# Attention scores in 128 + 128 + 32 contraction rows, queries laid out from PSUM, high half of P copied from the f32 P

## The chip, the cores and the metric

The kernel runs on one core of a Trainium2 chip, as one launch. The metric is the device time of that launch in microseconds: a median over runs. For the kernel before it is 1063.67 us, of three runs between 1063.38 and 1064.74.

## What is computed

Two layers act on x (2 batches x 512 tokens x 1024, f32) with a context of 2 x 1024 x 1024: a quantised matmul with the context, a linear layer with a low-rank update, cross-attention with 16 query heads over 4 key heads, and a router with an expert bias. The change touches the attention alone, in which B = 2, 512 queries and 1536 keys (1024 of the context, 512 latents) per batch, KV = 4 key heads, G = 4 query heads for each of them, HD = 96:

```python
hidden = jnp.concatenate([context, latents], axis=1)
q = (latents @ Wq.T).reshape(b, q_len, H, HD)
k = (hidden @ Wk.T).reshape(b, s_len, KV, HD)
v = (hidden @ Wv.T).reshape(b, s_len, KV, HD)
...
scores = jnp.einsum('bkgqd,bksd->bkgqs', q, k) * scale
attn = jax.nn.softmax(scores.astype(jnp.float32), axis=-1).astype(q.dtype)
out = jnp.einsum('bkgqs,bksd->bkgqd', attn, v)
```

Every f32 matmul is made of f16 products: each operand is split into a high half (its f16 rounding) and a low half (what is left, as f16), and high x high, high x low and low x high are summed in PSUM.

## The kernel before

The five engines each run a program written out by hand, joined by semaphores. The first 333 us prepare context, the first layer, and the keys and values, which lie in DRAM scratch (`k_scratch` with high and low halves of K transposed, `v_scratch`). Then comes the attention loop, `for m in range(NU)` with NU = 128 units in 8 stages of 16. A stage t is one pair of key head and batch (g = t // 2, b = t % 2); a unit u = m % 16 within it is one tile of 128 queries (u // 4) and one query head (u % 4), against all 1536 keys. The whole order is by hand.

**TensorE** (loop at L860): per unit `scores(m)` (L787), then at most one side product into bank 7, then `weigh(m - LAG)` (L802), P·V of the unit three before, into bank 6. The scores of even units lie in banks 0 to 2, of odd units in 3 to 5. Scores are nine matmuls (L798) of 96 contraction rows and 512 columns: three combinations of halves in three banks. P·V is 24 matmuls (L813, L815): twelve of 192 columns, twelve of 96. Side products: half of a q product for the next stage, 12 matmuls (L772), at u = 4, 5, 8, 9, 10, 11, of which u = 5, 9 and 11 end a block j = 0, 1, 2; an output product, 9 matmuls, at u = 2, 3, 6, 7, 12 to 15; none at u = 0 and 1. In the first stage the q products are at u = 2 (whole), 4, 5, 7, 8, there are value products at u = 0 and 1, and output products only from u = 12. In the last stage there are no q products, and the router and expert work is put in. Before a side product, `side_free` (L848) waits until bank 7 has been read, for q on `q_free`, the subtraction of the low half.

**VectorE** (loop at L1648): per unit `row_max(m)` (L1558), the reciprocal of the row sum of m - 3 (L1562), `take_low_q` where a q block ended, `add_out` (L1552) where there was an output product, then `take_out(m - 3)` (L1572, L1574), which reads bank 6 after P·V and frees it: `weigh(m)` waits for `o_ok >= m`, that is for `take_out(m - 1)`.

**ScalarE** (loop at L1238): per unit the f32 exponential from PSUM into p32 (L1249, row sums on the side, `e32_ok`), `take_q` where a q block ended (L1191), the same exponential again from PSUM as f16, the high half p_hi (L1259, `exp_ok`), and copies of weights. **GpSimd** (loop at L1848): per unit p_lo = p32 - p_hi (L1723, `plo_ok`), plus low halves of weights at u = 7 to 10 and 12 to 15 of every other stage and of the outputs. **SyncE** (loop at L508): per unit the two transposing DMAs of P (L517, L519), and at u = 1 the loads of K (`load_k`, L446) and V (L451) of the next stage.

q comes out of its product as a block j of 128 rows: rows 0 to 95 are head j, rows 96 to 127 the j-th third of head 3 (`q_rows`, L301). `take_q` writes the high half of both parts, `take_low_q` (L1540) subtracts it from PSUM and writes the low half; both lie in `q_head[rows, batch, head, half, query]`. The scores wait for a whole stage of q (`q_free`), for K, and, from m = 2, for `exp_ok >= m - 1`: the unit before the last in the same banks has been read for the second time.

## Time and profile before

| | |
|---|---|
| median of the runs | 1063.67 us |
| the profiled execution, its own time | 1062.25 us |
| its span, first to last instruction | 1060.5 us |
| attention loop, about | 333 to 1036 us of the span |
| TensorE busy | 1038.3 us (98%) |
| VectorE, ScalarE, GpSimd busy | 641.5, 635.6, 644.3 us |

Times in rows are microseconds from the start of the span, except mean durations in ns. PE is TensorE, DVE is VectorE, ACT is ScalarE, POOL is GpSimd, SPq the queue of SyncE, which issues the DMAs. A matmul's recorded duration reaches beyond the start of the next one, since they are pipelined; the spacing of starts is what a matmul costs. A timeline row that says x9 covers nine instructions.

### The profile page before, as it was taken

What the parts mean: (1) busy time and instruction counts of PE and PEld (TensorE: products, weight loads), DVE (VectorE), ACT (ScalarE), POOL (GpSimd) and SP (SyncE); (2) the same over time, 40 slices, a digit from 0 to 9 for tenths busy, and PEclk for the clock granted to TensorE, in tenths of its full rate; (3) what the DMA queues carried; (4) which work ended last, traced back from release to release, by engine and by line L of the source; (5) the groups of instructions that cost most, each with busy time, mean ns of one, the idle gap of its engine ahead of it and who ended that gap; (6) DMA issues with size and microseconds to landing.
All of it is one profiled execution on the core that took longest, in us unless ns stands there. A gap on an engine that the chain in (4) does not pass through costs nothing.

```text
span 1060.5 us, 18394 instructions
## 1 busy us (share of the span) xinstructions
PE 1038.3 (98%) x7262; PEld 586.4 (55%) x7262; DVE 641.5 (60%) x1092; ACT 635.6 (60%) x711; POOL 644.3 (61%) x348
## 2 busy tenths in 40 slices
PE   9999999999999999999999999999999999998987
PEld 4555444444545556566665655656656565565553
DVE  6989849644223565556556655654655655566767
ACT  5686535431224687665667756657766566677764
POOL 4476778242001589666677865668866667687771
PEclk9999999999999999999999999999999999999999
DMA  9986664843223999999999999899999999999995
GB/s 339 257 306 214 199 212 116 183 81 60 73 88 106 163 214 213 208 214 160 193 179 198 165 234 174 159 210 173 176 214 209 157 195 180 138 177 198 172 195 159
DMA packets 516570, 192.46 MB, mean 181 GB/s; under 512 B 484916, under 2 KB 500148, under 8 KB 516484
## 3 DMA queue, kind: packets, MB, share of 16 engines
q1 hardware_dynamic: 516484, 191.28, 87.5%
q8 instruction: 58, 0.95, 0.4%
q14 instruction: 28, 0.23, 0.1%
HBM read 56.88 MB, written 13.63 MB: 66 GB/s over the span
## 4 chain that ended last, share of the span: by engine, by line
PE 84%; DMA 4%; POOL 4%; DVE 3%; ACT 2%; issue 1%; SPq 1%; DVEq 0%; POOLq 0%
PE ps L556 34%; PE ps L798 20%; PE ps L772 11%; PE ps L813 10%; PE ps L815 5%; DMA region_o<-region_y 1%; DMA ln_t<-stage 1%; DVE p_max L1558 1%; POOL region_y L1723 1%; PE ps L578 1%; POOL x_res L1723 1%; POOL region_c L1723 1%; SPq L517 1%; DMA stage<-ctx_t_in 1%; POOL stage L1723 1%
## 5 line engine op out<-in xcount | busy, mean ns | idle before, releaser
L1723 POOL TENSOR_TENSOR region_y<-p,region_b 128x1536 f16<-128x1536 f32 x128 | 396.9, 3101 | 272.8 <-ACT region_b L1259 257.5
L1249 ACT ACTIVATE p<-ps,p_max 128x1536 f32<-128x1536 f32 x128 | 197.2, 1541 | 197.1 <-DVE p_max L1558 196.9
L1558 DVE TENSOR_REDUCE p_max<-ps 128x1 f32<-128x1536 f32 x128 | 224.9, 1757 | 113.8 <-PE ps L798 113.7
L798 PE MATMUL ps<-region_q,region_c 96*128 96x512 f16 x1152 | 269.8, 379 | 0.0
L813 PE MATMUL ps<-region_q,region_c 128*128 128x192 f16 x1536 | 207.6, 246 | 4.5 <-DVE logit L1583 2.4
L1259 ACT ACTIVATE region_b<-ps,p_max 128x1536 f16<-128x1536 f32 x128 | 196.5, 1535 | 18.5 <-DMA region_c<-region_b 17.8
L815 PE MATMUL ps<-region_q,region_o 128*128 128x96 f16 x1536 | 202.3, 206 | 0.0
L798 PEld LDWEIGHTS ps<-region_q,region_c 96*128 96x128 f16 x1152 | 105.3, 98 | 108.0 <-ACT region_b L1259 0.9
L813 PEld LDWEIGHTS ps<-region_q,region_c 128*128 128x128 f16 x1536 | 150.2, 98 | 23.1 <-issue 4.9
L815 PEld LDWEIGHTS ps<-region_q,region_o 128*128 128x128 f16 x1536 | 150.2, 98 | 13.2
L556 PE MATMUL ps<-region_w,region_q 128*128 128x512 f16 x576 | 134.9, 379 | 2.3 <-DMA region_q<-region_q 1.6
L772 PE MATMUL ps<-ln_t,region_w 128*128 128x512 f16 x576 | 131.3, 379 | 0.0
L1572 DVE TENSOR_SCALAR region_q<-ps,den_inv 128x96 f32<-128x96 f32 x128 | 40.7, 318 | 104.4 <-PE ps L815 97.0
L556 PEld LDWEIGHTS ps<-region_w,region_q 128*128 128x128 f16 x576 | 55.7, 98 | 69.5 <-issue 2.4
L772 PEld LDWEIGHTS ps<-ln_t,region_w 128*128 128x128 f16 x576 | 56.3, 98 | 68.0
L556 PE MATMUL ps<-region_c,ln_t 128*128 128x512 f16 x384 | 83.0, 379 | 0.4 <-DMA ln_t<-region_q 0.4
L1544 DVE SCALAR_TENSOR_TENSOR region_c<-ps,region_c 96x512 f16<-96x512 f32 (+1 forms) x48 | 33.1, 690 | 58.5 <-ACT region_c L1191 57.8
L1723 POOL TENSOR_TENSOR region_c<-stage,region_c 128x1024 f16<-128x1024 f32 (+1 forms) x25 | 53.3, 2151 | 17.6 <-ACT region_c L986 17.6
L556 PE MATMUL ps<-region_w,region_c 128*128 128x384 f16 x384 | 63.2, 326 | 0.0
L556 PEld LDWEIGHTS ps<-region_c,ln_t 128*128 128x128 f16 x384 | 37.5, 98 | 45.9 <-issue 0.8
L1723 POOL TENSOR_TENSOR rstd<-var_c,mhalf 128x1 f32<-128x1 f32 x32 | 25.4, 792 | 59.2 <-DVE var_c L1325 59.2
L986 ACT ACTIVATE region_o<-ps 128x384 f16<-128x384 f32 (+1 forms) x40 | 20.9, 537 | 67.0 <-PE ps L556 62.7
(151 smaller groups left out, 1152.7 us busy)
## 6 DMA issues: line engine op xcount, KB each, us to landing
stage<-ctx_in SPq DMA_DIRECT2D x16, 512.0 KB, 4.9
stage<-ctx_t_in SPq DMA_DIRECT2D x15, 512.0 KB, 8.7
stage<-wq_in SPq DMA_DIRECT2D x16, 384.0 KB, 4.1
stage<-wo_in SPq DMA_DIRECT2D x16, 384.0 KB, 4.3
k_scratch<-region_o SPq DMA_DIRECT2D x12, 384.0 KB, 6.8
region_q<-k_scratch SPq DMA_DIRECT2D x8, 576.0 KB, 5.9
region_q<-v_scratch SPq DMA_DIRECT2D x8, 576.0 KB, 6.2
x_res<-x_in SPq DMA_DIRECT2D x8, 512.0 KB, 8.8
```

What stands on the lines that cost most here:

```text
L556: ins = nc.tensor.matmul(out, a, b, start=first and n == 0, stop=last and n == len(pairs) - 1)
L772: ins = nc.tensor.matmul(by_tile(bank(at)), a, x, start=c == 0 and n == 0, stop=c == NC - 1 and n == 2)
L798: ins = nc.tensor.matmul(bank(NSB * (m % 2) + sb_), q_head[0:HD, b, h, hq, qt * P:(qt + 1) * P], k_head[0:HD, b, hk, sb_ * 512:(sb_ + 1) * ...
L813: nc.tensor.matmul(bank(6, VW), pt_hi[:, m % PT, i, :], v_head[:, b, i, :], start=i == 0, stop=False, skip_group_check=True)
L815: ins = nc.tensor.matmul(bank(6, HD), pt_lo[:, m % PT, i, :], v_head[:, b, i, 0:HD], start=False, stop=i == NS - 1, skip_group_check=True)
L986: return nc.scalar.activation(out, in_, ACT.Copy)
L1249: nc.scalar.activation(p32[:, m % 2, :], rows, ACT.Exp, bias=p_max[:, m % 4:m % 4 + 1], accum_out=den[:, m % 4:m % 4 + 1]).then_inc(e32_ok, 1)
L1259: nc.scalar.activation(p_hi[:, m % 2, :], rows, ACT.Exp, bias=p_max[:, m % 4:m % 4 + 1]).then_inc(exp_ok, 1)
L1544: nc.vector.scalar_tensor_tensor(q_head[rows, t % B, h, LO, :], bank(at)[part, :], SCALE, q_head[rows, t % B, h, HI, :], ALU.mult, ALU.sub ...
L1558: nc.vector.reduce_max(p_max[:, m % 4:m % 4 + 1], rows, axis=AX, negate=True).then_inc(max_ok, 1)
L1572: nc.vector.tensor_scalar(o_part[:, :], bank(6, VW)[:, HD:VW], d, None, ALU.mult).then_inc(part_ok, 1)
L1723: return nc.gpsimd.tensor_tensor(out, a, b, op)
```

## The change

A unit's scores have 3 x 96 = 288 contraction rows. They are regrouped as 128 + 128 + 32: rows 96 to 127 of the first two groups hold low q rows 0 to 31 and 32 to 63 beside the same rows of high K, and the last 32 (low q rows 64 to 95 with high K) come apart. Of these, each of the three key banks has a copy of q and its own piece of K on another 32 partitions (`q_rest`, `k_rest`). In even units from m = 2 on, the 32-row matmuls of m and of m + 1 follow each other, those of m + 1 as the first of their sums. `take_q` writes the high half twice (two slots), `take_low_q` puts the low half of head j into a buffer `q_low` and spreads it with five copies of 32 partitions x 512 f16, seven for j = 2. `load_k` issues five DMAs. The high half of P is a copy of p32 rounded to f16, and what waited for `exp_ok` on TensorE waits for `e32_ok`. The host's part is as before.

```diff
-        q_head = view(region_c, 0, 8192).rearrange("p (b g h s) -> p b g h s", b=2, g=G, h=2)
+        q_head = view(region_c, 0, 8192).rearrange("p (b g n s) -> p b g n s", b=2, g=G, n=2)
+        q_low = view(region_c, 8192 + PT * SL + 4 * QG, QL)
...
-        k_head = view(region_q, 0, 4 * SL).rearrange("p (b h s) -> p b h s", b=2, h=2)
+        k_head = view(region_q, 0, 4 * SL).rearrange("p (b n s) -> p b n s", b=2, n=2)
+        k_rest = view(region_q, 6144, 2 * QL).rearrange("p (b s) -> p b s", b=2)
...
+        q_rest = (stage[:, :, 3 * D // 4:D].bitcast(F16),
+                  view(region_q, 14272, G * QL).rearrange("p (g s) -> p g s", g=G))
...
                 sp.dma_start(k_head[0:HD, b, :, :], src).then_inc(k_ld[b], 16)
+                src = k_dram[b, HI, g * HD:g * HD + 2 * HP, :].rearrange("(n d) s -> d n s", n=2)
+                sp.dma_start(k_head[HD:P, b, :, :], src).then_inc(k_ld[b], 16)
+                for r in range(NSB):
+                    src = k_dram[b, HI, g * HD + 2 * HP:(g + 1) * HD, r * 512:(r + 1) * 512]
+                    sp.dma_start(k_rest[HP * r:HP * (r + 1), b, :], src).then_inc(k_ld[b], 16)
...
+            def score_rest(m, start):
+
+                b, qt, h = m // UPS % B, m % UPS // G, m % G
+                for r in range(NSB):
+                    rows = slice(HP * r, HP * (r + 1))
+                    ins = nc.tensor.matmul(bank(NSB * (m % 2) + r), q_rest[b][rows, h, qt * P:(qt + 1) * P],
+                                           k_rest[rows, b, :], start=start, stop=not start)
+                return ins
+
             def scores(m):
...
-                    pe.wait_ge(k_ld[b], use(t, B))
-                    pe.wait_ge(q_free, 2 * NJ * (t + 1))
+                    pe.wait_ge(k_ld[b], 5 * use(t, B))
+                rest_behind = m < 2 or m % 2 == 0
+                if u < G:
+                    pe.wait_ge(q_set, NJ * t + min(u + 1, NJ))
                 if m >= 2:
-                    pe.wait_ge(exp_ok, m - 1)
-                for n, (hq, hk) in enumerate(((HI, HI), (HI, LO), (LO, HI))):
+                    pe.wait_ge(e32_ok, m - 1)
+                for n in range(2):
                     for sb_ in range(NSB):
-                        ins = nc.tensor.matmul(bank(NSB * (m % 2) + sb_), q_head[0:HD, b, h, hq, qt * P:(qt + 1) * P],
-                                               k_head[0:HD, b, hk, sb_ * 512:(sb_ + 1) * 512], start=n == 0, stop=n == 2)
+                        ins = nc.tensor.matmul(bank(NSB * (m % 2) + sb_), q_head[:, b, h, n, qt * P:(qt + 1) * P],
+                                               k_head[:, b, n, sb_ * 512:(sb_ + 1) * 512],
+                                               start=rest_behind and n == 0, stop=not rest_behind and n == 1)
+                if rest_behind:
+                    ins = score_rest(m, False)
+                    if m >= 2:
+                        if u + 1 < G:
+                            pe.wait_ge(q_set, NJ * t + min(u + 2, NJ))
+                        pe.wait_ge(e32_ok, m)
+                        score_rest(m + 1, True)
                 ins.then_inc(sc_ready, 1)
...
-            pe.wait_ge(exp_ok, NU - 1)
+            pe.wait_ge(e32_ok, NU - 1)
...
                 for h, rows, part in q_rows(j):
-                    nc.scalar.activation(q_head[rows, t % B, h, HI, :], bank(at)[part, :], ACT.Copy, scale=SCALE
+                    both = bank(at)[part, :].unsqueeze(1).broadcast_to((part.stop - part.start, 2, 512))
+                    nc.scalar.activation(q_head[rows, t % B, h, :, :], both, ACT.Copy, scale=SCALE
                                          ).then_inc(q_hi, 1)
...
-                nc.scalar.activation(p_hi[:, m % 2, :], rows, ACT.Exp, bias=p_max[:, m % 4:m % 4 + 1]
-                                     ).then_inc(exp_ok, 1)
+                act.wait_ge(e32_ok, m + 1)
+                copy(p_hi[:, m % 2, :], p32[:, m % 2, :]).then_inc(exp_ok, 1)
...
             def take_low_q(n, at):
                 t, j = n // NJ, n % NJ
-                for k, (h, rows, part) in enumerate(q_rows(j)):
-                    dve.wait_ge(q_hi, 2 * n + k + 1)
-                    nc.vector.scalar_tensor_tensor(q_head[rows, t % B, h, LO, :], bank(at)[part, :], SCALE,
-                                                   q_head[rows, t % B, h, HI, :], ALU.mult, ALU.subtract
-                                                   ).then_inc(q_free, 1)
+                own, last, rest = q_head[:, t % B, j, :, :], q_head[:, t % B, G - 1, :, :], q_rest[t % B]
+                first, second, third = (slice(HP * r, HP * (r + 1)) for r in range(NJ))
+                part = slice(HD, P)
+
+                def low(out, rows, hi):
+                    return nc.vector.scalar_tensor_tensor(out, bank(at)[rows, :], SCALE, hi, ALU.mult, ALU.subtract)
+
+                if n > 0:
+                    dve.wait_ge(q_set, n)
+                dve.wait_ge(q_hi, 2 * n + 1)
+                low(q_low[0:HD, :], slice(0, HD), own[0:HD, 0, :]).then_inc(q_free, 1)
+                dve.wait_ge(q_hi, 2 * n + 2)
+                slice_hi = last[HP * j:HP * (j + 1), 0, :]
+                low(last[part, j, :] if j < 2 else rest[third, G - 1, :], part, slice_hi).then_inc(q_free, 1)
+                dve.wait_ge(q_free, 2 * n + 1)
+                nc.vector.tensor_copy(own[part, 0, :], q_low[first, :])
+                nc.vector.tensor_copy(own[part, 1, :], q_low[second, :])
+                for r in (first, second, third):
+                    ins = nc.vector.tensor_copy(rest[r, j, :], q_low[third, :])
+                if j == 2:
+                    dve.wait_ge(q_free, 2 * n + 2)
+                    for r in (first, second):
+                        ins = nc.vector.tensor_copy(rest[r, G - 1, :], rest[third, G - 1, :])
+                ins.then_inc(q_set, 1)
```

## Rows read from the trace of the kernel before

**Rows 1.** The page: busy time of TensorE, and its granted clock in 40 slices

```profile
PE 1038.3 (98%) x7262; PEld 586.4 (55%) x7262; DVE 641.5 (60%) x1092; ACT 635.6 (60%) x711; POOL 644.3 (61%) x348
...
PEclk9999999999999999999999999999999999999999
```

**Rows 2.** Table by stage: us, busy us of PE, PEld, DVE, ACT, POOL, clock, DMA share

```profile
592.40:678.60 86.20, 86.20 (x672) 51.90 (x670) 49.45 (x78) 54.67 (x59) 54.66 (x22) 1.00 1.02 190
937.00:1036.00 99.00, 88.85 (x830) 55.72 (x828) 67.72 (x164) 71.72 (x84) 76.76 (x64) 1.00 1.06 188
```

**Rows 3.** Timeline of TensorE around a q unit (u = 5) of stage 3

```profile
616.01 2.75 PE L772 MATMUL ps<-ln_t,region_w 128*128 128x512 f16 x12
...
620.11 2.11 PE L798 MATMUL ps<-region_q,region_c 96*128 96x512 f16 x9
622.05 2.11 PE L556 MATMUL ps<-region_w,region_q 128*128 128x512 f16 x9
...
625.49 0.81 PE L798 MATMUL ps<-region_q,region_c 96*128 96x512 f16 x3
```

**Rows 4.** Timeline of TensorE: 64-row matmuls (L845) between 128-row ones, near the end

```profile
1049.17 0.38 PE L844 MATMUL ps<-region_s,w_exp 128*128 128x512 f16 x1
1049.48 0.39 PE L845 MATMUL ps<-region_b,w_exp 64*128 64x512 f16 x1
1049.80 0.39 PE L844 MATMUL ps<-region_s,w_exp 128*128 128x512 f16 x1
```

**Rows 5.** Timeline of VectorE in the same q unit

```profile
616.21 1.76 DVE L1558 TENSOR_REDUCE p_max<-ps 128x1 f32<-128x1536 f32 x1 [1.20 <-PE ps L798]
617.89 0.15 DVE L1562 RECIPROCAL den_inv<-den 128x1 f32<-128x1 f32 x1
620.15 1.41 DVE L1544 SCALAR_TENSOR_TENSOR region_c<-ps,region_c 96x512 f16<-96x512 f32 x2 [2.11 <-ACT region_c L1191]
...
621.95 0.32 DVE L1574 SCALAR_TENSOR_TENSOR region_c<-ps,den_inv,region_q 128x96 f32<-128x96 f32 x1
```

**Rows 6.** Timeline of ScalarE in the same q unit

```profile
618.01 1.54 ACT L1249 ACTIVATE p<-ps,p_max 128x1536 f32<-128x1536 f32 x1 [1.75 <-DVE p_max L1558]
...
619.54 1.20 ACT L1191 ACTIVATE region_c<-ps 96x512 f16<-96x512 f32 x2
620.76 1.54 ACT L1259 ACTIVATE region_b<-ps,p_max 128x1536 f16<-128x1536 f32 x1
```

**Rows 7.** Timeline of GpSimd in the same q unit

```profile
622.38 3.10 POOL L1723 TENSOR_TENSOR region_y<-p,region_b 128x1536 f16<-128x1536 f32 x1 [2.94 <-ACT region_b L1259]
```

**Rows 8.** Groups by line and shape: count, busy us, mean ns of one

```profile
L986 ACT ACTIVATE region_c<-stage 128x1024 f16<-128x1024 f32 x23 | 23.9, 1053 | 19.9 <-DVE stage L1462 15.2 <-DMA stage<-ctx_t_in 4.4
...
L1618 DVE CAST w_tok<-logit 128x64 f16<-128x64 f32 x2 | 0.4, 194 | 0.1
...
L1618 DVE CAST w_tok<-logit 128x128 f16<-128x128 f32 x1 | 0.2, 227 | 0.0
```

**Rows 9.** Timelines of VectorE and of GpSimd, 109 to 120 us

```profile
110.41 0.69 DVE L1355 TENSOR_SCALAR stage<-stage 128x1024 f32<-128x1024 f32 x1
111.13 2.73 DVE L1358 TENSOR_SCALAR region_q<-stage 128x1024 f16<-128x1024 f32 x1
...
110.94 10.65 POOL L1723 TENSOR_TENSOR x_res<-x_res,region_b 128x1024 f32<-128x1024 f32 x4 [12.77 <-ACT region_b L1042]
```

**Rows 10.** Timeline of TensorE, first stage, q block ending at u = 5

```profile
367.61 2.11 PE L798 MATMUL ps<-region_q,region_c 96*128 96x512 f16 x9
...
371.34 2.11 PE L798 MATMUL ps<-region_q,region_c 96*128 96x512 f16 x9
```

**Rows 11.** Timelines of SyncE and ScalarE, loads of K and V in stage 3

```profile
605.61 0.90 SPq L449 DMA_DIRECT2D region_q<-k_scratch  x1
...
607.12 2.37 SPq L517 DMA_TRANSPOSE region_c<-region_b  x1
...
614.72 1.54 ACT L1259 ACTIVATE region_b<-ps,p_max 128x1536 f16<-128x1536 f32 x1 [1.11 <-DMA region_c<-region_b]
```

More of the change, by code:

```diff
@@ L33 @@
 VW = 2 * HD
+HP = 32
 E, R = 3, 40
@@ L106, in flamingo @@
         q2 = region_q[:, :]
-        k_head = view(region_q, 0, 4 * SL).rearrange("p (b h s) -> p b h s", b=2, h=2)
-        v_head = view(region_q, 4 * SL, 2 * NS * VW).rearrange("p (b s w) -> p b s w", b=2, s=NS)
-        o_t = view(region_q, 13824, 2 * 2 * QG).rearrange("p (r h j q) -> p r h j q", r=2, h=2, j=NJ)
-        v_last = view(region_q, 13824, 2 * KV * VW).rearrange("p (k t w) -> p k t w", k=KV, t=2)
-        o_cast = view(region_q, 15360, 2 * QG).rearrange("p (h n) -> p h n", h=2)
-        o_part = view(region_q, 16128, HD, F32)
+        k_head = view(region_q, 0, 4 * SL).rearrange("p (b n s) -> p b n s", b=2, n=2)
+        k_rest = view(region_q, 6144, 2 * QL).rearrange("p (b s) -> p b s", b=2)
+        v_head = view(region_q, 7168, 2 * NS * VW).rearrange("p (b s w) -> p b s w", b=2, s=NS)
+        o_t = view(region_q, 11776, 2 * 2 * QG).rearrange("p (r h j q) -> p r h j q", r=2, h=2, j=NJ)
+        v_last = view(region_q, 11776, 2 * KV * VW).rearrange("p (k t w) -> p k t w", k=KV, t=2)
+        o_cast = view(region_q, 13312, 2 * QG).rearrange("p (h n) -> p h n", h=2)
+        o_part = view(region_q, 14080, HD, F32)
+        q_rest = (stage[:, :, 3 * D // 4:D].bitcast(F16),
+                  view(region_q, 14272, G * QL).rearrange("p (g s) -> p g s", g=G))
         y_buf = region_y[:, :].rearrange("p (b d) -> p b d", b=2)
@@ L209, in flamingo @@
         v_ld = [sem(f"v_ld{b}") for b in range(B)]
-        q_ready, q_hi, q_free = sem("q_ready"), sem("q_hi"), sem("q_free")
+        q_ready, q_hi, q_free, q_set = sem("q_ready"), sem("q_hi"), sem("q_free"), sem("q_set")
         sc_ready, max_ok, e32_ok, exp_ok, plo_ok, pv_ok = (
@@ L926, in _ @@
             out_last(2, 30, 1, (2,))
-            pe.wait_ge(exp_ok, NU)
+            pe.wait_ge(e32_ok, NU)
             expert_mix(5, 3, 0)
```

## The prediction, made before the changed kernel was run

> **What bounds the kernel now.** I read three views in this order. The page: TensorE is busy 98% of the span at a full granted clock [rows 1], 2.4 GHz, so a change can gain on TensorE's work, or lose by making TensorE wait. The table by stage: an attention stage (one key head, one batch, 16 units) lasts 86.2 us with TensorE busy for all of it, while VectorE has 49, ScalarE 55 and GpSimd 55 us; only the last stage, 99 us long, has 10 us of idle TensorE [rows 2]. The timeline of one unit: nine score matmuls take 1.94 us, 0.216 each, a side product of 12 and the P·V product together 4.10, so P·V is 1.50 [rows 3]. Around it stands a chain: scores, row maximum, exponential, with q's two ScalarE copies and two VectorE subtractions in it every few units [rows 5, 6], then the low half of P on GpSimd [rows 7]. It is hidden, but not by much. P·V of unit m-3 may start only once VectorE has taken the output of unit m-4 out of the one bank, and VectorE does that behind the q work. In the first stage, where the unit after a q unit has no side product, TensorE waits for just this: two scores starts lie 3.73 us apart instead of 1.94 + 1.50 = 3.44 [rows 10]. In the other stages the slack is one side product.
>
> **Score matmuls.** A pair of units now issues 18, 3.88 us. After: 12 of 128 rows, 2.59, and two trios of 32 rows. In rows 3 a matmul of 96 rows costs what one of 128 does, so rows are free. The nearest row for the groups is a 64-row matmul between 128-row ones: starts 0.31 to 0.32 apart instead of 0.216 [rows 4], so a change of row grouping costs 0.10, twice per pair. No row has matmuls side by side. Bounds for the six: 6 x 0.216 + 0.20 = 1.50 one after another, 2 x 0.216 + 0.20 = 0.63 if a trio runs as one. I take 0.63: disjoint rows and three banks leave a trio nothing to share. Pair: 3.22, gain 0.66; 64 pairs give 42 us, the other end a loss of 13. The Trainium skill ("TensorE: Matmul & The Clock Gate", Part 3) gives four such tiles 3.07 times the speed of one after another, and no run here shows it; a trio at 4 x 0.216 / 3.07 = 0.28 would make the gain 34 by an estimate from that page. The last stage is only partly TensorE's: I give it half of its 5.3, so **-39**.
>
> **The new wait in the middle of an even unit.** The 32-row part of m+1 waits until the f32 exponential of m-1 has emptied the banks. From TensorE's last score matmul of m-1 that is 0.20 to the maximum, 1.76, 1.54 and the accumulator and gaps, some 3.7 us [rows 5, 6]. TensorE has P·V 1.50, six matmuls 1.30 and 0.32 of the first trio: 3.12, plus a side product of 1.94 or 2.59. Behind u = 1 there is none, so u = 2 stalls 0.56 in seven stages, and u = 10 and 12 of the first stage: **+5**. Queued behind it are the side product and P·V, nothing that others miss.
>
> **High half of P from the f32 P.** ScalarE's copy of 1024 elements takes 1.05 [rows 8], of 512 about 0.60 (two in 1.20, rows 6), so of 1536 some 1.50, against 1.54 now. It now waits until the exponential and its row sums are out; 0.1 is my guess for that, as instructions follow each other there without a gap now (618.01 + 1.54 = 619.55, rows 6). Net nothing; hidden by ScalarE's 31 idle us in a stage [rows 2]. If that cover went, 128 x 0.06.
>
> **Queries.** This is the term that decides. Three units of a stage (u = 5, 9, 11) end a q block. In rows 3 to 7, with the side product of u = 5 starting at 616.01:
> - ScalarE's copies start at 619.54 and now write both slots, 1.03 instead of 0.60 each: done at 621.60, not 620.74.
> - VectorE's second subtraction (0.69) ends at 622.32, not 621.56. Bank 7 comes free with it. TensorE arrives there at 616.01 + 2.59 + 1.50 + 1.30 + 0.63 = 622.03 and starts its next side product at 622.37: 0.34 lost.
> - Then five copies (seven for the third block) of 32 x 512, f16 to f16. No row has one. Below: an instruction of one element, 0.15 [rows 5]; above: the cast of 128 elements at 0.227 and of 64 at 0.194 [rows 8], so 0.43 for 512. At the subtraction's rate it would be 0.69. I take 0.29, midway between 0.15 and 0.43, since no row has 16 bits on both sides.
> - ScalarE's copy of P ends at 623.10, and GpSimd starts its 3.10 us subtraction at 623.18 (now 622.38). In the first part of the kernel a TENSOR_SCALAR from SBUF to SBUF takes 0.69 while GpSimd is idle and 2.73 while GpSimd works through a queue [rows 9]: about one of GpSimd's (10.65 / 4 = 2.66), so each waits for the end of the other's. Between 622.35 and 623.18 three copies fit. The other two (four) wait until 626.3.
> - So VectorE ends the copies at 626.9 (627.5) and takes the output 0.71 later (as 621.56 to 622.27 now): 627.6 (628.2). TensorE wants it at 622.37 + 1.94 = 624.3, or + 2.59 = 625.0 behind u = 9. Stalls 3.3, 2.65 and 3.9, with 3 x 0.34: 10.9 a stage, six stages: **+65**.
>
> Whether a plain copy meets GpSimd as TENSOR_SCALAR does, no row tells. The Trainium skill ("SBUF — State Buffer", Who interferes with whom) names copy, cast and tensor_scalar together as taking the port pair that VectorE shares with GpSimd, and says the second to start is blocked for the whole instruction of the first; by it the stall above stands, and without it rival B would be the sum.
>
> In the first stage the q blocks end at u = 2, 5 and 8, with no side product behind. Behind u = 5 and 8 TensorE wants the output 6.0 and 5.4 us after the side product's start and gets it after 11.6 and 12.2, less the 0.29 that it waits already [rows 10]: 5.3 and 6.5. At u = 2 the product has 24 matmuls; counted from its start, ScalarE's copies end at 7.4, GpSimd's subtraction at 12.1, the two late copies at 12.7, maximum and exponential of unit 3 at 16.1, and TensorE wants that for unit 5 at 5.18 + 1.30 + 1.50 + 1.62 = 9.6: 6.5. Together **+18**.
>
> **Loads, joined banks, layouts.** Keys come in five DMAs instead of one and half as many bytes again. SyncE's one issue takes 0.90 now, and the transposes of P queue behind: the next is issued 1.5 after it, and ScalarE waits 1.11 for an earlier transpose to land [rows 11]. Four more issues of at most 0.90, up to 3.6 us, go ahead of the transposes of u = 2. P·V of u = 2 starts in u = 5, some 11 us later; 0 to 1.5 per stage, I take nothing, as it comes ahead of a stall that absorbs it. Moving views costs nothing. The tail's two waits on the f32 exponential come 1.5 earlier, behind no bound there.
>
> **Sum.** -39 + 5 + 65 + 18 = +49 on the profiled execution's 1062.25: 1111. The median is 1.4 above that execution: **1112 us**.
>
> **Rivals.**
> A, the forecast: copies meet GpSimd. Against it: all hangs on 0.83 us of room. At 0.15 a copy, five take 0.75 and pass, seven don't. Its own range: 1092 where the fourth and fifth copies slip in and only the third block collides in full, 1128 with copies of 0.43 and late loads.
> B, faster: the copies don't wait for GpSimd. Then they end at 623.8 (624.4), the output is out at 624.5 (625.1) and TensorE stalls 0.2, 0 and 0.8, with 1.0 for the bank: 2.0 a stage, 12; first stage 2.2 + 3.4 + 3.3, 9. -39 + 5 + 12 + 9 = -13, and 1.4 for the median: 1051. It decides at q's last copy. For it: no plain copy was ever seen waiting in this trace.
> C, trios run one after another: 55 us on top of A, less what the stalls shrink by, 1160. Against it: nothing in the rows; for it: no matmuls overlap here.
> D, everything added is hidden and TensorE keeps its gain: 1063.7 - 39 = 1025. Against it: the first stage's 0.29 shows that there the chain has no slack at all.
>
> **Numbers.** A 0.56, B 0.27, D 0.08, C 0.05, and 0.04 that gain and stall cancel within 0.2% (2 us, what a measurement of this kernel can tell). Slower is A and C, 0.61; faster B and D, 0.35. The range goes from B, with its stalls 9 us smaller, to A's upper end: 1042 to 1128.
>
> **What would show it.** Right: trios with starts nearly together and 0.3 before and after; TensorE idle 3 to 4 us ahead of P·V, three times a stage; VectorE's 32 x 512 copies bimodal, some 0.3 and some over 2; GpSimd's instruction inside the long ones; stages of some 92 us. Wrong: all copies short, or TensorE 100% busy in stages of 81 us, which is D; starts of the 32-row matmuls 0.216 apart is C. A granted clock that drops to 1.2 GHz behind the longer idle stretches would put the time above the range's middle.

## The result, and the profile after

The changed kernel takes **1137.89 us** (median of 4 runs, 1133.2 to 1141.92) beside 1064.2 of the kernel before: ratio **1.069**, 95% interval 1.0648 to 1.0734. The direction was the forecast one, the size was not: 1112 was said, 1128 was the upper end. The profiled execution has a span of 1137.0 us, 76.5 more than before. Rows of the page, with TensorE at 90% where it had 98 [rows 1], and with a clock that is no longer whole:

```profile
PE 1028.8 (90%) x7262; PEld 567.6 (50%) x7262; DVE 729.3 (64%) x1228; ACT 655.9 (58%) x711; POOL 644.1 (57%) x348
...
PEclk9999999999998889998998999999999999998999
```

The table by stage (columns as in [rows 2]) for the stages 3 and 4, from the first score matmul of a stage to that of the next:

```profile
631.47:721.16 89.69, 81.81 (x675) 47.61 (x673) 59.39 (x95) 57.45 (x61) 55.89 (x22) 1.00 1.02 180
721.16:819.73 98.57, 85.03 (x676) 49.93 (x673) 63.70 (x95) 61.95 (x67) 63.02 (x28) 0.97 0.90 172
```

TensorE has less to do than the 86.4 us of before (81.8 at full clock), but the stage is longer. The q work of [rows 3, 5, 7], here the third block of stage 2 (u = 11, with the scores of u = 12 at 605.49). TensorE:

```profile
605.49 1.46 PE L819 MATMUL ps<-region_q,region_c 128*128 128x512 f16 x6
606.88 0.61 PE L802 MATMUL ps<-region_q,stage 32*128 32x512 f16 x6
607.80 2.10 PE L566 MATMUL ps<-region_w,region_q 128*128 128x512 f16 x9 [0.31 <-issue]
613.44 0.26 PE L842 MATMUL ps<-region_q,region_c 128*128 128x192 f16 x1 [3.53 <-DVE region_c L1623]
...
615.51 2.56 PE L819 MATMUL ps<-region_q,region_c 128*128 128x512 f16 x6
```

VectorE:

```profile
607.00 0.70 DVE L1577 SCALAR_TENSOR_TENSOR region_q<-ps,region_c 32x512 f16<-32x512 f32 x1 [0.28 <-ACT region_c L1221]
607.73 0.29 DVE L1587 COPY region_c<-region_c 32x512 f16<-32x512 f16 x1
608.03 0.29 DVE L1588 COPY region_c<-region_c 32x512 f16<-32x512 f16 x1
608.33 3.75 DVE L1590 COPY region_q<-region_c 32x512 f16<-32x512 f16 x3
612.10 0.58 DVE L1594 COPY region_q<-region_q 32x512 f16<-32x512 f16 x2
...
613.06 0.32 DVE L1623 SCALAR_TENSOR_TENSOR region_c<-ps,den_inv,region_q 128x96 f32<-128x96 f32 x1
```

GpSimd:

```profile
608.55 3.09 POOL L1772 TENSOR_TENSOR region_y<-p,region_b 128x1536 f16<-128x1536 f32 x1 [1.12 <-ACT region_b L1015]
```

Two copies take 0.29. Of the next three one runs into GpSimd's subtraction, and they end 0.44 us behind it, at 612.08. Over all, one line of copies has a median of 0.28 us and a longest of 3.17, from the trace by source line:

```profile
L1590 DVE COPY region_q<-region_c x36: 281/284/3172, 356.9 to 991.0; 32x512 f16<-32x512 f16 x36
```

Behind the copies VectorE takes the P·V output (L1623, 613.06), and TensorE waited 3.53 us for that. The windows of that wait and of what follows it show the second half of the price:

```profile
609.90:613.44 3.54, 0.01 (x2) 0.01 (x1) 3.43 (x7) 0.00 (x0) 1.74 (x1) 1.00 0.93 188
613.44:617.91 4.47, 4.47 (x31) 2.93 (x31) 2.96 (x5) 2.74 (x3) 0.00 (x0) 0.62 0.67 153
617.91:621.35 3.44, 3.44 (x34) 2.37 (x33) 2.58 (x3) 2.56 (x4) 2.99 (x1) 1.00 0.58 108
```

Behind the idle stretch the granted clock is 0.62 over 4.47 us, most of it at 1.2 GHz. Six score matmuls take 2.56 us there (615.51) and 1.46 at 605.49.

Of the 18 q blocks of the stages 1 to 6, 14 end in such a wait of 2.3 to 3.65 us, 45.7 us in all. Behind ten of the 14 the clock falls, behind four it stays at 1.00. That gives its price within this one trace. At u = 12 the wait is 3.53 or 3.54 us in the stages 2 to 6, and TensorE has the same 87 matmuls in the two units from there. In the stages 2, 4 and 6 the clock falls and they take 15.84 to 15.86 us; in 3 and 5 it doesn't and they take 14.19. The difference, 1.66 us, is all in TensorE's busy time (stage 2, then stage 3 with its wait):

```profile
605.49:621.35 15.86, 12.02 (x87) 6.73 (x85) 12.47 (x19) 8.23 (x9) 8.02 (x4) 0.89 0.76 161
696.85:711.04 14.19, 10.34 (x87) 5.88 (x85) 12.39 (x19) 7.45 (x8) 6.00 (x4) 1.00 0.61 117
```

```profile
704.79 0.26 PE L842 MATMUL ps<-region_q,region_c 128*128 128x192 f16 x1 [3.54 <-DVE region_c L1623]
```

Over the ten such pairs of units TensorE's busy time is some 18 us more than in pairs at full clock. Why the clock fell behind these ten waits and not behind the other four (2.81 us twice, 3.53 and 3.54) stays open.

Where GpSimd happens to be late (a transpose had not landed), the copies get through: at u = 9 of stage 3 all five took 0.29 us.

### The profile page after: what moved, and what is told of

It reads as the page before. It is cut to its first block, busy times and chain, and to the rows that moved or that the text cites. A ratio compares the mean times of both kernels' runs of the same rounds, so it can differ in the third digit from the quotient of the medians.

```text
span 1137.0 us, 18750 instructions
## 1 busy us (share of the span) xinstructions
PE 1028.8 (90%) x7262; PEld 567.6 (50%) x7262; DVE 729.3 (64%) x1228; ACT 655.9 (58%) x711; POOL 644.1 (57%) x348
## 3 DMA queue, kind: packets, MB, share of 16 engines
q1 hardware_dynamic: 518276, 193.64, 81.8%
## 4 chain that ended last, share of the span: by engine, by line
PE 53%; DVE 15%; DMA 9%; ACT 7%; issue 6%; POOL 5%; SPq 5%; DVEq 0%; ACTq 0%; POOLq 0%
PE ps L566 27%; PE ps L819 7%; PE ps L842 6%; DVE p_max L1607 4%; DVE region_q L1590 4%; PE ps L782 4%; POOL region_y L1772 4%; DMA region_c<-region_b 4%; ACT p L1279 3%; PE ps L844 3%; DMA region_o<-region_y 3%; DVE stage L1590 2%; ACT region_c L1221 2%; SPq L529 2%; DMA ln_t<-stage 2%
## 5 line engine op out<-in xcount | busy, mean ns | idle before, releaser
L842 PE MATMUL ps<-region_q,region_c 128*128 128x192 f16 x1536 | 221.4, 255 | 66.5 <-DVE region_c L1623 58.6
L844 PE MATMUL ps<-region_q,region_o 128*128 128x96 f16 x1536 | 216.2, 213 | 0.0
L1015 ACT ACTIVATE region_b<-p 128x1536 f16<-128x1536 f32 x128 | 189.7, 1482 | 41.5 <-DMA region_c<-region_b 32.8
L842 PEld LDWEIGHTS ps<-region_q,region_c 128*128 128x128 f16 x1536 | 155.5, 101 | 96.1 <-DVE region_c L1623 69.9
L819 PE MATMUL ps<-region_q,region_c 128*128 128x512 f16 x768 | 196.8, 395 | 0.0
L844 PEld LDWEIGHTS ps<-region_q,region_o 128*128 128x128 f16 x1536 | 155.3, 101 | 9.9
L819 PEld LDWEIGHTS ps<-region_q,region_c 128*128 128x128 f16 x768 | 71.0, 102 | 67.2 <-issue 10.4
L782 PEld LDWEIGHTS ps<-ln_t,region_w 128*128 128x128 f16 x576 | 55.2, 99 | 77.0 <-issue 15.6
L1577 DVE SCALAR_TENSOR_TENSOR region_c<-ps,region_c 96x512 f16<-96x512 f32 (+1 forms) x40 | 27.6, 691 | 77.8 <-ACT region_c L1221 77.7
L1601 DVE SCALAR_TENSOR_TENSOR x_res<-ps,tg,x_res 128x512 f32<-128x512 f32 x64 | 47.7, 746 | 20.7 <-PE ps L566 17.9
```

The costliest lines, as they stand in the source:

```text
L782: ins = nc.tensor.matmul(by_tile(bank(at)), a, x, start=c == 0 and n == 0, stop=c == NC - 1 and n == 2)
L819: ins = nc.tensor.matmul(bank(NSB * (m % 2) + sb_), q_head[:, b, h, n, qt * P:(qt + 1) * P], k_head[:, b, n, sb_ * 512:(sb_ + 1) * 512], s ...
L842: nc.tensor.matmul(bank(6, VW), pt_hi[:, m % PT, i, :], v_head[:, b, i, :], start=i == 0, stop=False, skip_group_check=True)
L844: ins = nc.tensor.matmul(bank(6, HD), pt_lo[:, m % PT, i, :], v_head[:, b, i, 0:HD], start=False, stop=i == NS - 1, skip_group_check=True)
L1015: return nc.scalar.activation(out, in_, ACT.Copy)
L1601: nc.vector.scalar_tensor_tensor(xh, bank(at), tg[:, 1:2], xh, ALU.mult, ALU.add).then_inc(wo_free, 1)
```

## The experiments

Stage lengths in us, by the first score matmul of each stage; "tail" is from the first one of the last stage to the end of the span, where the text uses it:

```
                  stage 0  1     2     3     4     5     6     1 to 6   tail
before             82.7   87.9  86.4  86.4  86.4  86.4  86.4   519.8   124.7
after             105.8   92.0  99.4  89.7  98.6  96.1  94.9   570.6   126.3
e1 no copies      104.3   85.0  83.8  85.3  84.9  84.1  83.3   506.4
e3 on ScalarE      92.6   86.2  87.4  86.1  88.6  87.9  86.7   523.0
e10 short reads    92.3   84.8  85.0  86.7  85.5  86.5  85.6   514.0
e15 first apart    86.2   86.1  85.1  86.9  85.5  86.6  85.9   516.0
e14 loads earlier  86.6   86.8  84.8  85.9  84.2  86.1  84.0   511.9
e16 fewer at once  85.6   87.6  82.9  85.2  83.8  86.4  82.6   508.6
e18 before+copies  95.9   99.1 100.2  95.9  98.6  95.9  95.5   585.2   128.6
```

**e1, no copies from the second stage on.** The loop's copies are left out behind block 6, and TensorE waits for `q_free` in their place.

```
+                if n >= 2 * NJ:
+                    return
                 dve.wait_ge(q_free, 2 * n + 1)
                 nc.vector.tensor_copy(own[part, 0, :], q_low[first, :])
```

> The changed kernel, in which the 32x512 copies of the low queries are made for the first six blocks only; from the second stage on none is made, so that the output is not the reference's (the scores of the later stages multiply old values, in the same number of matmuls). Theory 1 (VectorE's copies run into GpSimd's subtraction, hold the reading of the P.V bank up, and TensorE waits for it three times a stage, and then runs for some us at 1.2 GHz): the six middle stages, 570.6 us now, go to the 86.4 us of before less 4.9 us of saved matmuls and plus some 1.5 us, 83 us each, and the time to about 1065 us; no wait of P.V on VectorE over 1 us behind the first stage. Theory 2 (the longer ScalarE reads of the queries and the wait of the joined group cost it): within 15 us of the changed kernel, over 1120 us. Theory 3 (the matmuls of 32 rows cost TensorE more than they save): the stages stay over 90 us with no waits in them.

1073.4 us, ratio 1.009 (1.0063 to 1.011): 64.5 us less than the changed kernel, all in the stages 1 to 6, where no P·V waits for VectorE for over 1 us. Theories 2 and 3 fall. The stages take 84.4 on average, not 83: TensorE idles 16.6 us in the six, where it idled 1.1 before: 0.9 us at u = 6 and 0.3 to 0.6 at u = 10 and 12 ahead of the side product, 0.2 to 0.5 at u = 2 for the exponential that the joined group waits for (the six 32-row matmuls of two units), up to 1.3 for a transposed low half of P.

**e2, copies behind the reading of the P·V bank.**

```
                 if m >= LAG:
                     take_out(m - LAG)
+                if q_end(m) is not None:
+                    spread_q(NJ * (t + 1) + q_end(m))
```

> The changed kernel with the copies of the low queries behind the reading of the P.V bank (take_out) of the same unit on VectorE, in place of ahead of it. Theory 1: the copies still meet GpSimd (some of 2 to 3 us), but P.V no longer waits 3.5 us for them; what is late is the next unit's row maximum by up to 3 us, which the exponential and the wait of the joined group on it feel: some 1 us per block. 1065 to 1085 us. Theory 2 or 3: no more than 10 us faster than the changed kernel, since the copies are still made.

1134.35 us, ratio 1.068 (1.0617 to 1.0734). Theory 1's own number was wrong by 50 us, and the other theories' number, no more than 10 us faster than the changed kernel, is what came. e1 rules those theories out, and by the rows the copies still hold TensorE up, elsewhere. VectorE, then TensorE:

```profile
604.49 0.32 DVE L1629 SCALAR_TENSOR_TENSOR region_c<-ps,den_inv,region_q 128x96 f32<-128x96 f32 x1
604.84 0.29 DVE L1593 COPY region_c<-region_c 32x512 f16<-32x512 f16 x1
605.14 3.08 DVE L1594 COPY region_c<-region_c 32x512 f16<-32x512 f16 x1
...
609.73 1.76 DVE L1613 TENSOR_REDUCE p_max<-ps 128x1 f32<-128x1536 f32 x1
```

```profile
601.49 0.39 PE L802 MATMUL ps<-region_q,stage 32*128 32x512 f16 x3 [1.71 <-ACT p L1279]
...
604.21 2.29 PE L566 MATMUL ps<-region_w,region_q 128*128 128x512 f16 x5 [2.33 <-DVE region_q L1577]
```

The bank of P·V is read in time, and the copies, as long as before, hold up the next row maximum, and with it what stands behind it: the joined group waits for its exponential (1.71 us here), and a side product for bank 7, which the subtraction reads late at u = 12 (2.33) and `add_out` at u = 7 (up to 3.05). In both places that were tried somebody waits behind the copies.

**e3, the copies on ScalarE**, behind its copy of P (`act.wait_ge(q_free, 2 * n + 2)`, then the same five or seven as `copy`).

> The changed kernel with the copies of the low queries, those of the loop, on ScalarE behind the high half of P of the same unit. Theory 1: five copies of about 0.5 us on an engine that shares nothing with GpSimd (if it does, one of them shows 3 us here too), no wait of P.V for VectorE over 1 us; the copy of p_hi of the next unit 2.5 us later, with three units of room. 1060 to 1080 us, the first stage too shorter. Theory 2 (ScalarE's time is what decides): slower than the changed kernel or no faster than by 10 us, over 1128 us.

1076.52 us, ratio 1.011 (1.0092 to 1.0128). Each copy takes 0.63 us, and none is long:

```profile
L1015 ACT ACTIVATE region_c<-region_c x42: 627/627/629, 356.3 to 932.0; 32x512 f16<-32x512 f16 x42
```

So it is not the copy but the engine pair. All copies are made here, and 61 of the 74 us are gone. The stages 1 to 6 are still 16.6 us longer than in e1. What is left: 3.98 and 3.79 us in the first stage for an exponential, and 1.96 us at u = 12 of the even stages for GpSimd's low half of the weights (L1791), for which ScalarE's copies had come ahead.

**e4, the high half of P alone**, in the kernel before.

```
-                nc.scalar.activation(p_hi[:, m % 2, :], rows, ACT.Exp, bias=p_max[:, m % 4:m % 4 + 1]
-                                     ).then_inc(exp_ok, 1)
+                act.wait_ge(e32_ok, m + 1)
+                copy(p_hi[:, m % 2, :], p32[:, m % 2, :]).then_inc(exp_ok, 1)
```

> The kernel before, with one part of the change alone: the high half of P is a copy of the f32 P, and the scores wait for the first exponential in place of the second one. Theory 1: ScalarE's instruction keeps its length (1.48 in place of 1.54 us), nothing waits less: within 2 us of the kernel before. Rival: this part alone takes a wait away and gains 5 us or more, or the copy from SBUF meets VectorE and costs 5 us or more.

1066.14 us, ratio 1.0017 (1.0006 to 1.0029): some 2 us slower, as good as nothing.

**e5 and e13, work in the waits.** e5 computes the side products of u = 6, 10 and 12 twice. e13 has matmuls that nobody waits for, ahead of P·V:

```
+                if alone(m) and t < TS - 1:
+                    keep_clock(m + 1, 12)
...
+            def keep_clock(m, n):
+                b, qt, h = m // UPS % B, m % UPS // G, m % G
+                pe.wait_ge(e32_ok, m - 1)
+                for i in range(n):
+                    nc.tensor.matmul(bank(NSB * (m % 2) + i % NSB), q_head[:, b, h, 0, qt * P:(qt + 1) * P],
+                                     k_head[:, b, 0, 0:512], start=True, stop=True)
```

> The changed kernel with more work for TensorE where it waits: from the second stage on the side products of u = 6, 10 and 12 are computed twice, the second time over the first (9, 12 and 9 matmuls, 1.94, 2.59 and 1.94 us at full clock, 38.8 us over the six stages), just ahead of the 18 waits of 2.3 to 3.65 us for the P.V bank. If a wait costs only its own length, the time stays at 1138 us (within 4 us). If the wait also brings the 1.2 GHz stretches behind it (granted clock 0.95 to 0.97 in five of the six stages, 19 us lost when summed over them), the clock stays at 1.00 there and the time falls to 1118 to 1125 us although more is computed. If TensorE were the bound, it would be 1177 us.

> The changed kernel in which TensorE multiplies during the waits: at u = 6, 10 and 12 of the stages 1 to 6, between the side product and P.V, it makes 12 more score matmuls (2.56 us at full clock, 46 us in all) into banks that nobody reads before they are written anew, and the 32-row groups of these units are not joined (18 more changes of rows, about 6 us). Nothing that VectorE waits for comes later, unlike in busy_wait. If the 1.2 GHz stretches cost what the sums of granted clock say (19 us), the time is 1137.9 + 6 - 19 = 1125 us, within 5; if they cost nothing beside the waits, 1144 us.

e5: 1137.16 us; e13: 1141.0, ratios 1.0697 and 1.0721. Both totals are near those that I had put down for a slow clock that costs nothing (1138 and 1144), and not near the forecast ones (1118 to 1125, and 1125). But the clock is 1.00 in the stages 1 to 6 of both, for instance in e5

```profile
721.00:820.00 99.00, 92.66 (x740) 53.29 (x738) 64.05 (x100) 64.86 (x69) 66.03 (x28) 1.00 0.95 175
```

The totals hide two things that cancel, which the pairs of units from u = 6, 10 and 12 of the six stages show apart. In the ten pairs in which the clock had fallen in the changed kernel, e13 is 10.9 us shorter (152.5 against 163.4), though it computes twelve matmuls more in each. In the other eight, of which four had no wait at all, it is 13.1 longer (116.0 against 102.9): there the added matmuls cost time and had no clock to win back. In e5 it is 13.5 shorter and 9.2 longer. The forecasts had taken the added work to be free everywhere. So the slow stretches were time lost, by e13 at least 1.1 us each, and some 1.7 by the comparison within the changed kernel.

**e6, e7, e8, the copies as DMAs.** e6: five, five and seven DMAs from SyncE behind the unit's transposes. e7: ScalarE's reads of q at 512 columns as before, and two more DMAs. e8: e7 with `rest_behind = True` for every unit.

> The changed kernel with the copies of the low queries of the loop made by 5, 5 and 7 DMAs from SyncE, behind the transposes of the same unit. Theory 1: VectorE carries no copies, the first stage included: 1050 to 1062 us (the run without copies from the second stage on, 1073, less 10 to 20 in the first stage); the stages near 84.5 us. Rival: the DMAs make the transposes of P late, P.V waits for them in place: 1075 us or more.

> The run before (copies_dma) in which ScalarE writes the high half of the queries once (512 columns, about 0.60 us each in place of 1.02), and two more DMAs a block make its second place. Theory 1: bank 7 is read 0.85 us earlier, so the 0.9 us for which the output product at u = 6 starts late is gone, one or two us a stage less: 1038 to 1052 us. Rival: the size of ScalarE's reads does not matter, within 2 us of copies_dma.

> The run before (all_dma) with the 32-row matmuls of each unit behind its own 128-row ones, three and three, not six for two units. Theory 1: a change between 128 and 32 rows costs TensorE about 0.1 to 0.3 us each, and there are twice as many: 10 to 20 us more than all_dma, though the waits of the joined group for the exponential of the unit just before (4 us and more in the first stage) are gone. Rival: joining buys less than its wait costs: not slower than all_dma.

1097.61, 1123.26 and 1123.9 us (ratios 1.032, 1.056, 1.056). Theory 1's numbers failed in all three. The rivals of e6 and e8 were right; that of e7, within 2 us of e6, was not. SyncE's queue in e7:

```profile
606.55 0.58 SPq L530 DMA_DIRECT2D region_c<-region_c  x1
607.18 0.59 SPq L531 DMA_DIRECT2D region_c<-region_c  x1
607.81 1.91 SPq L533 DMA_DIRECT2D region_q<-region_c  x3
...
612.99 1.46 SPq L550 DMA_TRANSPOSE region_c<-region_b  x1
614.49 2.79 SPq L552 DMA_TRANSPOSE region_o<-region_y  x1
```

Each DMA of 32 KB holds the queue for 0.6 us. Nine are 5.7 us, a whole unit in which no transpose of P goes out, and P·V waits up to 6.0 us for `region_o`. A second wait comes from the buffer: VectorE may write `q_low` anew only when the DMAs of the block before have landed, in stage 2 of e7

```profile
595.60 0.69 DVE L1612 SCALAR_TENSOR_TENSOR region_c<-ps,region_c 96x512 f16<-96x512 f32 x1 [6.28 <-DMA region_c<-region_c]
```

and TensorE, which wants bank 7 read for the side product of u = 12, stands still for 3.7 us. On joining: where nothing waits at u = 14 and 15, a pair takes 10.78 us before, 10.12 in the changed kernel and 10.33 in e8 (stages 3, 5 and 6), so joining is worth 0.21 a pair. That the totals are equal means that it went into waits: in the stages 1 to 6 TensorE is busy for 5.5 us more in e8 than in e7 (512.6 and 507.1) and idle for 6.1 less (49.1 and 55.2).

**e9 and e10, ScalarE again, at most three copies a unit**, behind the weights' copies; e10 reads q at 512 columns and fills the second place by two copies later.

```
+                if q_end(m) is not None:
+                    moves.append(spread_q(NJ * (t + 1) + q_end(m)))
+                move_some()
```

> The changed kernel with the copies of the low queries of the loop on ScalarE (0.63 us each there), three in a unit behind the copies of weights, over the units that follow a block, in place of five to seven at once ahead of the weights. Theory: copies_scalar (1076.5 us) still waited 2 to 3.3 us at u = 12 of the stages 2, 4 and 6, for GpSimd's low half of the weights, because ScalarE's copies came ahead of the weights' high half; with that gone 1066 to 1072 us. Rival: three copies a unit make ScalarE late in every one of those units (1.9 us more on some 4.3 us of work in a unit of 5.4), and it is 1076 us or more.

> The run before (spread) with ScalarE's reads of the queries from PSUM at 512 columns (some 0.60 us each in place of 1.02), the second place of the high half filled by two more copies later. Theory: the units 6, 10 and 12 of a middle stage, which take 6.35, 6.40 and 5.75 us in the run without copies where the same matmuls would allow 5.4, 6.0 and 5.4, lose 0.85, 0.4 and 0.3 us of that, since bank 7 is read earlier: 5 to 10 us less than spread. Rival: what is late there is another thing than bank 7, within 2 us of spread.

1070.95 and 1068.66 us (1.0044 to 1.0088 and 1.0024 to 1.0059). e9 is what was said. e10 is 2.3 us faster, not 5 to 10, and the intervals overlap: unit 6 of stage 2 falls from 6.36 to 5.71 and unit 10 from 6.40 to 6.03, as expected, but ScalarE, with two copies more, loses part of it elsewhere.

**e11, e12, e14, e15, the K loads and the first stage.** e11 is e10 with the four added loads at u = 7, 12, 13, 14; e12 is e11 with the first stage's groups not joined; e14 is e12 with the loads at u = 2, 7, 8, 12; e15 is e12 with all of them at u = 1, as in the change.

```
+        K_LOAD = {7: 1, 12: 2, 13: 3, 14: 4}
...
+                if u in K_LOAD and 0 < t < TS - 1:
+                    load_k(t + 1, K_LOAD[u])
...
-                rest_behind = m < 2 or m % 2 == 0
+                rest_behind = m < UPS or m % 2 == 0
```

> The run before (short_reads) with the four extra loads of K of a stage issued at u = 7, 12, 13 and 14, one each, in place of all at u = 1. Theory: each DMA holds the queue of the transposes for about 0.6 us, so four in a row delay the transposes of u = 2 by 2.4 us, for which P.V waits about 0.2 to 1.7 us a stage; apart they fit in: 2 to 6 us less than short_reads. Rival: the queue has room anyway, within 1 us.

> The run before (loads_apart) with the 32-row matmuls of the first stage's units each behind their own, not two units together. Theory: there the joined group waits for the exponential of the unit just before, which take_q and take_low_q hold up (3.98 and 3.79 us in copies_scalar): 4 to 8 us less than loads_apart, and with it the whole under the kernel before, 1045 to 1058 us. Rival: the wait moves to the next unit, less than 2 us.

> The run first_apart (1089.9 us) with the four extra loads of K of a stage issued at u = 2, 7, 8 and 12 in place of 7, 12, 13 and 14. Theory: the 4.7 to 6.1 us that the first scores of each stage waited for k_scratch there go, with the slow clock behind them, 6.4 us in each of six stages: 1050 us, within 6, under the kernel before. Rival: the load at u = 12 is still late, over 1070 us.

> The run short_reads (1068.7 us) with the 32-row matmuls of the first stage's units each behind their own; the loads of K all at u = 1 as in the change. Theory: first stage 6 to 7 us shorter, as between loads_apart and first_apart; the rest as short_reads: 1062 us, within 4. Against loads_earlier it tells what the four loads in a row cost: 2 to 12 us in all if the queue of the transposes feels them, nothing if not.

1094.54, 1089.92, 1057.75 and 1062.71 us. e15 is what was said; e14 misses its range by 1.8 us; the totals of e11 and e12 miss theirs by over 20. e11 was a mistake of placing that says something by itself: the load issued at u = 14 lands too late, each stage from stage 2 on begins with a wait, and then with a slow clock (six matmuls in 2.74 us):

```profile
606.65 2.74 PE L840 MATMUL ps<-region_q,region_c 128*128 128x512 f16 x6 [5.82 <-DMA region_q<-k_scratch]
```

Not joining the first stage gives 6.0 us in e15 against e10, as said, and 4.6 in e12 against e11. e14 against e15: the four loads in a row cost 5.0 us, 4.1 of them in the stages 1 to 6.

**e16, e17, ScalarE less full; e18, the copies alone in the kernel before.**

```
-                move_some()
+                move_some(2 if u in (5, 6, 7, 8, 10) else 3)
```

e17 moves the load of V to u = 2 and the added loads of K to u = 7, 8, 11 and 12. e18 adds to the kernel before, behind each low query block:

```
+                    for i in range(5 if j < 2 else 7):
...
+                        nc.vector.tensor_copy(spare[32 * slot:32 * (slot + 1), :], q_head[0:32, t % B, j, LO, :]).then_inc(cp, 1)
```

> The run loads_earlier (1057.8 us) with at most two of ScalarE's copies at u = 5, 6, 7, 8 and 10, three elsewhere. Theory: in the stages 2, 4 and 6 the output product at u = 12 begins 1.4 us late because ScalarE, three copies behind the weights and the outputs at u = 10, reads the last query block late; a stall of 0.3 to 0.8 us at u = 4 to 6 of the next exponential goes as well: 2 us a stage, 1047 to 1055 us. Rival: it only moves, within 2 us of loads_earlier.

> The run before (fewer_at_once) with the load of V at u = 2 in place of u = 1 and the four extra K loads at u = 7, 8, 11 and 12. Theory: at u = 2 of the stages P.V waited 1.2 to 1.8 us for the transposed low half behind two loads; 1 to 2 us a stage less. Rival: V at u = 2 makes the same wait one unit later, within 2 us.

> The kernel before, to which nothing is added but the change's copies: behind each low query block of the loop, 5, 5 and 7 copies of 32x512 f16 on VectorE from the low queries into a place that nobody reads. Theory: they run into GpSimd as in the change and hold up the reading of the P.V bank and the next row maximum: between the changed kernel and its copy without them lie 64.5 us in six stages, and the first stage, with its units so dense, gives some 15 to 20 more: 1130 to 1150 us. Rival: without the longer reads of ScalarE ahead of them the copies finish before GpSimd begins, and it stays under 1090 us.

e16: **1052.45 us, ratio 0.989 (0.9871 to 0.9902)**, 11.7 us under the kernel before, the best version. e17: 1053.83, no different, as its rival had it. e18: **1140.48 us, ratio 1.072 (1.0693 to 1.074)**. The copies alone, with nothing else of the change, cost 76 us, as much as the whole change. VectorE, GpSimd and TensorE of e18:

```profile
605.06 4.96 DVE L1555 COPY region_c<-region_c 32x512 f16<-32x512 f16 x7
610.05 0.32 DVE L1582 TENSOR_SCALAR region_q<-ps,den_inv 128x96 f32<-128x96 f32 x1
```

```profile
605.84 3.09 POOL L1733 TENSOR_TENSOR region_y<-p,region_b 128x1536 f16<-128x1536 f32 x1 [2.19 <-ACT region_b L1260]
```

```profile
610.78 0.26 PE L814 MATMUL ps<-region_q,region_c 128*128 128x192 f16 x1 [3.16 <-DVE region_c L1584]
```

Seven copies are 7 x 0.28 = 2.0 us of work and take 4.96. A stage of e16, beside 86.4 us before:

```profile
505.74:588.68 82.94, 81.41 (x675) 47.88 (x673) 49.09 (x78) 71.50 (x86) 61.43 (x27) 1.00 1.07 196
```

## Why the prediction was right in kind and short in size

The difference of 76.5 us of span is 1.0 ahead of the first stage, 23.1 in it, 50.8 in the stages 1 to 6 and 1.6 behind. The forecast's terms give 13.8, 37.0 and -2.1 for the last three, 48.7.

In the stages 1 to 6 the forecast's 37.0 is 59 of P·V waits, 9.5 of other gaps and -31.7 of score matmuls. The 50.8 measured are 45.7 of P·V waits, 14.4 of other gaps (15.5, of which 1.1 were there before), 19.6 of slow clock, and -28.9 of score matmuls by TensorE's busy time. So the clock is more than the 13.8 that are missing there, and it is partly luck that the total came as near as it did: four blocks slipped past GpSimd.

- **Score matmuls, -39: right.** A pair of units lost 0.66 us (10.78 to 10.12), 0.66 was said. Trios run as one: three 32-row matmuls show 0.39 us together (e2's row at 601.49), and one has a median of 0.38; the second trio starts 0.23 us behind the first. Six of them with both changes of rows cost 3.88 - 0.66 - 2.59 = 0.63, as taken. In the Trainium skill ("TensorE: Matmul & The Clock Gate", Part 3) four such tiles are 3.07 times as fast as one after another, for which the prediction had 0.28 a trio, an estimate from that page, and so 0.76 for the six; this trace is faster than that.
- **Queries, ten-odd us a stage: the right mechanism.** Copies of 0.28 where 0.29 was taken; longest 3.17; ScalarE's reads 1.02 for 1.03; waits at u = 6, 10 and 12 of stage 2 of 2.81, 3.65 and 3.53 us where 3.3, 2.65 and 3.9 stood. By e1 the copies behind the first stage cost 64.5 us, and by e3 the same copies on another engine cost 16.6 of the stages 1 to 6 (523.0 against 506.4). The Trainium skill ("SBUF — State Buffer", Who interferes with whom) has VectorE's copies and GpSimd behind one pair of ports, the second to start blocked for the whole instruction of the first; by that rule the trace agrees, and ScalarE's copies, which it leaves out of the lock, stayed at 0.63 us beside GpSimd. Two things were not in the sum: 4 of 18 blocks slipped through, and the stall at u = 10 of the stages 2, 4 and 6 is 3.65 where it is 2.30 in stage 5, since there the fifth copy takes 1.63 us beside GpSimd's low half of a weight.
- **The step that failed: a stall was priced at its own length.** The sum had TensorE go on at full speed behind each. The clock fell to 1.2 GHz behind most of them: TensorE's busy time in the stages 1 to 6 is 509.4 us against 489.8 in e1 with the same matmuls, 19.6 more, and by an estimate some 7 in the first stage (84.6 us busy, where seven joined pairs at 0.66 leave 77.8 of the 82.4 before). The forecast fell 26 us short; that these two make about that is in part chance, as above. The last paragraph of the prediction named the fall of the clock and gave it no term. Within the changed kernel a wait with the fall costs 1.66 us more than the same wait without it, some 18 of the 19.6 lie behind the ten waits with it, and e5 and e13 show that the clock stays up when TensorE is given work.
- **First stage, +18: the waits right.** 6.17, 5.36 and 7.52 us where 6.5, 5.3 and 6.5 stood, and one of 1.53 more. What was missed there is the clock, 0.89 over the stage.
- **New wait of the joined group, +5: about right in the middle stages**, 0.2 to 0.5 us at u = 2 in e1 for 0.56. In the first stage it weighs more, since the exponential of the unit just before stands behind the q work: e15 against e10 gives 6.0 us without joining there, copies on ScalarE given.
- **Loads, nothing: wrong.** They cost 5.0 us with the copies on ScalarE (e15 against e14), between the 0 and the 1.5 a stage of the bounds. In the changed kernel no stall absorbs them either: P·V waits for a transpose at u = 5, 0.38 us in stage 2 and 1.45 in stage 4, and the stall at u = 6 behind it is 2.81 in both.
- **High half of P, nothing: right within some 2 us** (e4), 1.48 us for 1.50.
- **Tail.** -2.1 was said and +1.6 measured. At u = 2 of the last stage the router's product waits 3.06 us for a transposed tile, where the wait was 0.9. No run was made on that, and it stays open.
- **The rivals.** B (copies pass GpSimd, 1051) fell at q's last copy, as the text had it. That e16 stands at 1052 doesn't speak for its number: e16 also has other loads, shorter reads and an unjoined first stage, and with the copies moved to ScalarE and nothing else e3 stands at 1076.5. C fell with the trios' rows. D fell.

## What to carry to other kernels

A copy of 0.28 us on VectorE costs up to GpSimd's whole instruction, here 3.1 us, if GpSimd is working in SBUF; moving it within VectorE's order did not help, since there too somebody waited behind it, and moving it to ScalarE did. When TensorE is 98% busy, price a stall at its length and, where the clock may fall behind it, at some 1.7 us more; here it fell behind ten of 14 stalls of 2.3 to 3.65 us. An added DMA costs the queue it is put on (0.4 to 0.9 us for a load of K here, 0.6 for a copy within SBUF), so place it by what stands behind it in that queue and by when it must have landed, at both ends.

## What the runs showed of the hardware that was not expected

- TensorE could be given 38.8 us more matmuls at the same total time (e5): they kept the clock at 1.00 and filled waits, which made up for what they cost where there was neither.
- A DMA of 32 KB from SBUF to SBUF mostly lands 1.9 to 2.5 us after its issue and holds SyncE's queue 0.6 us (e7). A transposing DMA of P holds it 1.35 us at least, 1.7 to 1.8 at the median and up to 4.7.
- In 0.3 to 1.0 us ahead of some side products TensorE waits for nothing that the profile shows ("issue"). Where ScalarE's reads of bank 7 were shortened (e10), unit 6 of stage 2 went from 6.36 to 5.71 us, so most of the 0.9 there is a wait for the bank.
